# Third layer of a four-layer graph network: how the gathered rows are weighed, and how the ring that holds them is freed

## The chip, the cores and the metric

The kernel runs on one core of one Trainium2 chip. The metric is the device time of one execution in microseconds (us); the kernel before takes 5078.98 us, the median of three runs between 5077.45 and 5080.45. The engines are called by the names of the profile: PE is TensorE (PEld its weight loads), DVE is VectorE, ACT is ScalarE, POOL is GpSimd, SP is SyncE. "DVEq" is the part of VectorE that handles waits, registers and semaphores ahead of the arithmetic.

## The reference

3125 nodes with 128 features go through four graph layers over 50000 edges. The change touches the first half of the third layer, attention with eight heads of 64 features:

```python
def gat_layer(x, W, a, src, dst, n_nodes, concat):
    h = x @ W
    f = h.shape[-1]
    s_src = h @ a[:f]
    s_dst = h @ a[f:]
    score = s_src[src] + s_dst[dst]
    edge_e = jnp.exp(-jax.nn.leaky_relu(score, ALPHA))
    rowsum = jax.ops.segment_sum(edge_e, src, num_segments=n_nodes)
    msg = jax.ops.segment_sum(edge_e[:, None] * h[dst], src, num_segments=n_nodes)
    h_prime = msg / (rowsum[:, None] + EPS)
    return jax.nn.elu(h_prime) if concat else h_prime

heads = [gat_layer(x, W1[i], a1[i], src, dst, N, True) for i in range(W1.shape[0])]   # 8 heads
x_ = jnp.concatenate(heads, axis=1)
h = gat_layer(x_, W2, a2, src, dst, N, False)
```

For each edge the row h[dst] of every head is fetched, multiplied by that head's exp(-leaky_relu(score)), and added to the sums of node src. A column of ones in each head's row lets the same sum give the row sum: 8 x 65 = 520 values are summed, and eight values s_dst ride along, so that a record has 528 float32.

## The kernel before

The 3125 nodes are padded to 25 blocks of 128. An earlier stage has sorted the edges into a table of 416 slot rows of 128 lanes each (`SLOT_ROWS` = 416): in a slot row every lane holds one edge, and all of them belong to one block of nodes, whose number stands in `chunk_row`. `attend_rows` goes through this table once, in one block in which the five engines run side by side and wait for each other by semaphores. Within an engine the order is the one that the Python text writes out; there is no planner.

- POOL (L2053) gathers one slot row after the other by an indirect DMA into `got`, a ring of 3 buffers of 13 rows. Before it refills a buffer it waits (`free`) until DVE has added the whole set of 13 rows that lay in it.
- DVE makes the logits of a set of 13 rows in `leak` (L2127, L2128), after a wait for all 13 gathers; ACT takes the exponential (L2186); DVE multiplies by `live` in `mask` (L2135), which zeroes empty lanes. The results are the weights `factor`, in SBUF.
- Each row is then weighed in place: ACT multiplies heads 0 and 1, one ACTIVATE each (L2204), and DVE heads 2 to 7 in one operation of 390 values (L2142, `scale`). DVE adds the weighed row of 520 values to the block `y` that the row's chunk number selects (L2166). The add waits for the row's two multiplications (`scaled`, `weighed`) and for the add before it (`added`), because two rows can go to the same block.
- DVE's order is: scale of row t+1, add of row t, scale of row t+2, add of row t+1, and so on. `leak` of the next set stands before row 7 of a set, `mask` before row 12. At the start of each set `reg_load` (L2150) fetches 13 chunk numbers from `chunk_row` into registers; it follows a wait for all adds of the set before.
- Beside this, the same block transposes a matrix of edge counts for later layers: SP fetches pieces of `ct` (800 KB each, 25 of them), PE transposes 128x128 blocks (L2090) and counts degrees (L244), ACT copies each transposed strip out of PSUM (L2193, `flip`, one after every third row, 125 in all), and SP stores 25 pieces to `cs`. In ACT's order a flip stands between the rows, so an ACT that waits for PE in a flip does not weigh rows.

The first layer's rounds (L1607, L1664, L1673, L1681, L1698) do a similar job on rows of 516 values, with other lines of code: a ring freed by eights, register loads of eight, and adds that follow each other directly. They are not touched.

Part of the weighing in the text before:

```python
for r in range(ROWS):
    t = n * ROWS + r
    if n + 1 < SETS and r == 7:
        leak(n + 1)
    if n + 1 < SETS and r == ROWS - 1:
        mask(n + 1)
    if t + 1 < SLOT_ROWS:
        scale(t + 1)
```

## Time and profile before

| | |
|---|---|
| Median of three runs | 5078.98 us (5077.45 to 5080.45) |
| The profiled execution, its own time | 5069.63 us |
| Its span | 5067.9 us |
| Busy in the span | PE 1669.7, DVE 2841.0, ACT 1640.9, POOL 2024.4 us |
| The stage of the change, first gather to last add | 3448.8 to 4125.2 us |

The profile comes from one execution that is a little faster than the median. The stage of the change fills slices 28 to 33 of its 40, where DVE, ACT and POOL are all partly busy and PE's granted clock is at its lower level. A row of the timeline gives the start of an operation, its duration, engine, line, what it writes and reads, and in brackets the engine's idle time before it with the releaser that the profile infers; "issue" as releaser means that the engine waited for nothing that the profile shows, so a register load is hidden behind that word. Durations of neighbouring operations on DVE overlap a little; what an operation costs its engine is the distance from its start to the next start.

### The profile page before, as it was taken

Reading aid. Unit: us, or ns where it says so; the run is one execution under the profiler, and the core shown is the slowest. Engines: PE = TensorE matmul, PEld = TensorE weight load, DVE = VectorE, ACT = ScalarE, POOL = GpSimd, SP = SyncE. Lnnn points to the kernel's source line nnn. Section 1 sums busy time; section 2 is a strip of 40 time slices with the busy share of each in tenths; the row PEclk is TensorE's granted clock in tenths of the full one; section 3 lists DMA queues with packets and bytes.
Section 4 is the critical chain, followed back from the end, with each engine's and each line's share of the span. In section 5 each row is a group of like instructions: output and inputs, shape, how many; then the busy total and the mean of one; then the engine's idle time right before and its main releaser. Section 6 shows DMA issues by size and latency. Waiting matters only on the chain. (4 is left out here: it accounts for less than half of the span.)

```text
span 5067.9 us, 46827 instructions
## 1 busy us (share of the span) xinstructions
PE 1669.7 (33%) x10711; PEld 944.4 (19%) x10711; DVE 2841.0 (56%) x4778; ACT 1640.9 (32%) x4317; POOL 2024.4 (40%) x1847
## 2 busy tenths in 40 slices
PE   3133200100000000001543433522222237899989
PEld 2022200100000000000111111111111127644444
DVE  5728667781677779871333333564777775722131
ACT  1312301110656657001544333513444454310010
POOL 0055777706777710027123444126767642000000
PEclk9566555555555555555666665665555568999999
DMA  3000000005666620002011122226778736578856
GB/s 120 19 12 1 3 1 1 1 0 163 169 181 186 185 49 0 0 20 51 17 38 44 54 59 56 51 72 199 246 233 251 239 78 178 193 278 271 269 169 211
DMA packets 215383, 553.41 MB, mean 109 GB/s; under 512 B 46177, under 2 KB 112411, under 8 KB 214404
## 3 DMA queue, kind: packets, MB, share of 16 engines
q0 software_dynamic: 99984, 272.83, 19.9%
q1 hardware_dynamic: 115188, 278.18, 16.1%
q8 instruction: 82, 1.34, 0.1%
q14 instruction: 129, 1.06, 0.1%
HBM read 485.70 MB, written 65.20 MB: 109 GB/s over the span
## 5 line engine op out<-in xcount | busy, mean ns | idle before, releaser
L1171 POOL DMA_INDIRECT blend_got<-rec,blend_slot x416 | 394.8, 949 | 539.7 <-DVEq L1214 407.4
L900 POOL DMA_INDIRECT table<-edges_record,edges_place x391 | 512.8, 1311 | 142.9 <-issue 123.6
L2691 PE MATMUL fourth_bank<-fourth_tile,fourth_z 128*128 128x512 f16 (+1 forms) x2800 | 559.8, 361 | 19.8 <-DVEq L2852 10.1
L2053 POOL DMA_INDIRECT heads_got<-rec,heads_slot x416 | 466.8, 1122 | 183.8 <-issue 124.4
L244 PE MATMUL blend_count<-blend_mov,blend_stat 128*128 x980 | 351.2, 440 | 562.0 <-issue 461.6
L1607 POOL DMA_INDIRECT sum_got<-rec,sum_slot x416 | 456.9, 1098 | 157.3 <-issue 124.9
L1223 DVE TENSOR_SCALAR blend_mov<-built_iota_low,built_low 128x800 f16 x490 | 213.0, 435 | 516.2 <-issue 318.0
L1681 DVE TENSOR_TENSOR rounds_y<-rounds_y,sum_got 128x516 f32 x416 | 290.9, 699 | 124.7 <-issue 34.8
L1251 ACT ACTIVATE blend_gap<-built_iota_ten,built_offset 128x128 f32 x490 | 196.8, 402 | 493.4 <-issue 392.4
L200 PE MATMUL edges_p_key<-kept_ident,edges_key_row 128*128 128x128 f32 x4 | 1.1, 428 | 1035.6 <-DVEq L167 1035.6
L2691 PEld LDWEIGHTS fourth_bank<-fourth_tile,fourth_z 128*128 128x128 f16 x2800 | 261.7, 99 | 311.6 <-issue 15.0
L2166 DVE TENSOR_TENSOR third_a_y<-third_a_y,heads_got 128x520 f32 x416 | 288.6, 694 | 53.1 <-issue 35.1
L2142 DVE TENSOR_TENSOR heads_got<-heads_got,heads_factor 128x390 f32<-128x390 f32 x416 | 232.8, 560 | 111.8 <-issue 102.6
L1698 ACT ACTIVATE sum_got<-sum_got,edges_place 128x129 f32<-128x129 f32 x672 | 198.7, 387 | 265.2 <-issue 208.3
L244 PEld LDWEIGHTS blend_count<-blend_mov,blend_stat 128*128 x980 | 99.7, 102 | 822.1 <-issue 799.2
L2204 ACT ACTIVATE heads_got<-heads_got,heads_factor 128x65 f32<-128x65 f32 x832 | 217.2, 340 | 91.8 <-DVEq L2136 53.6
L1211 DVE SCALAR_TENSOR_TENSOR second_sums<-blend_got,blend_weight,second_sums 128x129 f32 x416 | 126.8, 351 | 157.3 <-issue 138.0
L1698 ACT ACTIVATE sum_got<-sum_got,sum_weights 128x129 f32<-128x129 f32 x576 | 169.4, 388 | 110.5 <-issue 55.1
L200 PEld LDWEIGHTS edges_p_key<-kept_ident,edges_key_row 128*128 128x128 f32 x4 | 0.7, 217 | 1036.3 <-issue 1036.3
L477 PE MATMUL once_bank<-kept_ident,once_e_rows 128*128 128x128 f32 x200 | 41.9, 393 | 421.4 <-issue 264.3
L1253 ACT ACTIVATE blend_stat<-blend_gap x490 | 151.6, 309 | 89.5 <-issue 39.8
L244 PE MATMUL heads_degrees<-heads_one,heads_flipped 128*128 128x1 f16 x625 | 41.0, 170 | 386.1 <-issue 162.4
(666 smaller groups left out, 4394.7 us busy)
## 6 DMA issues: line engine op xcount, KB each, us to landing
fourth_tile<-cs SPq DMA_DIRECT2D x100, 800.0 KB, 4.4
fourth_tile<-ct SPq DMA_DIRECT2D x100, 800.0 KB, 4.3
ct<-blend_cst SPq DMA_DIRECT2D x20, 1000.0 KB
heads_counts<-ct SPq DMA_DIRECT2D x25, 800.0 KB
cs<-heads_flipped SPq DMA_DIRECT2D x25, 800.0 KB
attend_cnt<-ct SPq DMA_DIRECT2D x50, 256.0 KB
sort_low_wide<-low SPq DMA_DIRECT2D x4, 3136.0 KB
attend_cnt<-ct SPq DMA_DIRECT2D x25, 288.0 KB
```

What stands on the lines that cost most here:

```text
L244: return pe.matmul(out, lhsT, rhs, start=False, stop=True, skip_group_check=True)
L900: pool.indirect_dma_start(table, bass.IndirectOffsetOnAxis(ap=K["place"][0:lanes, t:t + 1], axis=0), K["record"][0:lanes, t, :], None).the ...
L1171: pool.indirect_dma_start(got[:, buf, r, :], None, rec_dram, bass.IndirectOffsetOnAxis(ap=slot[:, t:t + 1], axis=0)).then_inc(gathered[buf ...
L1223: dve.tensor_scalar(at_slot(mov, at), K["iota_low"][:, :], K["low"][:, bass.ds(t, 1)], None, ALU.is_equal).then_inc(mov_ready, 1)
L1607: pool.indirect_dma_start(got[:, t % (HELD * PART), :], None, rec_dram, bass.IndirectOffsetOnAxis(ap=slot[:, t:t + 1], axis=0)).then_inc(g ...
L1681: dve.tensor_tensor(sums, sums, got[:, t % (HELD * PART), 0:heads * F1], ALU.add).then_inc(added, 1)
L1698: last = act.activation(part, part, ACT.Copy, scale=weights[half][:, k, r:r + 1])
L2053: pool.indirect_dma_start(got[:, buf, r, :], None, rec_dram, bass.IndirectOffsetOnAxis(ap=slot[:, t:t + 1], axis=0)).then_inc(gathered[buf ...
L2142: dve.tensor_tensor(part, part, factor[:, buf, r, ON_ACT:heads].unsqueeze(2).to_broadcast([P, heads - ON_ACT, F1]), ALU.mult).then_inc(sca ...
L2166: dve.tensor_tensor(out, out, got[:, buf, r, 0:WIDTH], ALU.add).then_inc(added, 1)
L2204: last = act.activation(part, part, ACT.Copy, scale=factor[:, buf, r, h:h + 1])
L2691: last = pe.matmul(bank[m][:, 0:w], z2[s % 2][:, k, part, :], tile[:, n % RING, at:at + w], start=(k == 0 and part == 0), stop=(k == NB - ...
```

## The change

- The ring becomes one of 40 rows in 5 parts of 8. POOL waits, before each part from the sixth on, for `added` to show that the part's old rows are summed; there is no `free` semaphore any more.
- A set is 16 rows (25 of them, and two of 8 at the end) instead of 13. `leak` has one add for each part of 8 rows and then the leaky step over the set; it stands before row 9 of a set of 16, `mask` before row 14.
- ACT weighs heads 0 to 2 (three ACTIVATEs for each row), DVE heads 3 to 7 of two rows in one operation of 650 values. `mask` is two operations: the weights of ACT's heads go to `factor` in SBUF as before, those of DVE's heads go to `across`, a part of the PSUM bank `p_slot`. `scale` reads its weights from there.
- DVE's order becomes: scale of rows r+2 and r+3, add of row r, add of row r+1.
- `reg_load` fetches 8 chunk numbers at every eighth row, and no wait for the adds stands before it.

```diff
-    BUFS, ROWS = 3, 13
-    SETS = SLOT_ROWS // ROWS
-    ON_ACT = 2
+    PART, HELD, ROWS = 8, 5, 16
+    SETS = [ROWS] * 25 + [PART, PART]
+    FIRST = [sum(SETS[:n]) for n in range(len(SETS))]
+    KEPT = 3
+    ON_ACT = 3
...
+    there = heads - ON_ACT
+    across = p_slot[:, 0:KEPT * ROWS * there].rearrange("p (u r h) -> p u r h", u=KEPT, r=ROWS)
...
-            for n in range(SETS):
-                buf = n % BUFS
-                if n >= BUFS:
-                    pool.wait_ge(free[buf], n // BUFS)
...
+            for part in range(SLOT_ROWS // PART):
+                if part >= HELD:
+
+                    pool.wait_ge(added, (part - HELD + 1) * PART)
+                for t in range(part * PART, (part + 1) * PART):
...
-                step(dve.tensor_tensor(l, own[:, :, at].rearrange("p h r -> p r h"), got[:, buf, :, WIDTH:WIDTH + heads], ALU.add))
+                l = logit[:, n % 2, 0:rows, :]
+                for part in range(first // PART, (first + rows) // PART):
+                    wait_gathered(dve, part)
+                    at = slice(part * PART, (part + 1) * PART)
+                    step(dve.tensor_tensor(l[:, part * PART - first:(part + 1) * PART - first, :], own[:, :, at].rearrange("p h r -> p r h"),
+                                           got[:, held(part * PART, PART), WIDTH:WIDTH + heads], ALU.add))
...
+                step(dve.tensor_tensor(e[:, :, 0:ON_ACT], e[:, :, 0:ON_ACT], alive.to_broadcast([P, rows, ON_ACT]), ALU.mult))
                 dve.sem_inc(factors, 1)
+                step(dve.tensor_tensor(across[:, n % KEPT, 0:rows, :], e[:, :, ON_ACT:heads], alive.to_broadcast([P, rows, there]), ALU.mult))
+
+            def scale(n, r):
+
+                part = got[:, held(FIRST[n] + r, 2), ON_ACT * F1:WIDTH].rearrange("p r (h f) -> p r h f", f=F1)
+                dve.tensor_tensor(part, part, across[:, n % KEPT, r:r + 2, :].unsqueeze(3).to_broadcast([P, 2, there, F1]),
+                                  ALU.mult).then_inc(scaled, 2)
...
+            for n, rows in enumerate(SETS):
+                for r in range(rows):
+                    t = FIRST[n] + r
+                    if r % PART == 0:
+                        dve.reg_load(regs, chunk_row[0:1, t:t + PART])
+                    if n + 1 < len(SETS) and r == rows - 7:
                         leak(n + 1)
+                    if n + 1 < len(SETS) and r == rows - 2:
                         mask(n + 1)
+                    if r % 2 == 0 and r + 2 < rows:
+                        scale(n, r + 2)
+                    elif r % 2 == 0 and n + 1 < len(SETS):
+                        scale(n + 1, 0)
...
-                    dve.wait_ge(scaled, t + 1)
+                    dve.wait_ge(scaled, t // 2 * 2 + 2)
                     dve.wait_ge(weighed, t + 1)
                     if t >= 1:
                         dve.wait_ge(added, t)
...
-                dve.wait_ge(added, (n + 1) * ROWS)
-                dve.sem_inc(free[buf], 1)
+            dve.wait_ge(added, SLOT_ROWS)
...
-                if n >= BUFS:
-                    act.wait_ge(free[n % BUFS], n // BUFS)
+                rows = SETS[n]
+                if n >= KEPT:
+                    act.wait_ge(added, FIRST[n - KEPT + 1])
...
-                    if n + 1 < SETS and r == 9:
+                    if n + 1 < len(SETS) and r == rows - 5:
                         exps(n + 1)
```

## Rows read from the trace of the kernel before

**Rows 1.** Stage's middle: busy us of PE, PEld, DVE, ACT, POOL; clock; DMA share.
```profile
3504.00:4091.00 587.00, 134.66 (x1790) 101.65 (x1790) 439.89 (x842) 266.08 (x913) 426.66 (x377) 0.50 0.79 240
```

**Rows 2.** Groups of instructions, 3440 to 4130 us: busy and mean ns, idle before.
```profile
L2053 POOL DMA_INDIRECT heads_got<-rec,heads_slot x416 | 466.8, 1122 | 183.8 <-issue 124.4 <-DVEq L2168 51.3 <-DVEq L2113 8.1
L2166 DVE TENSOR_TENSOR third_a_y<-third_a_y,heads_got 128x520 f32 x416 | 288.6, 694 | 53.1 <-issue 35.1 <-ACT heads_got L2204 16.9 <-DVE third_a_y L2166 0.2
L2142 DVE TENSOR_TENSOR heads_got<-heads_got,heads_factor 128x390 f32<-128x390 f32 x416 | 232.8, 560 | 111.8 <-issue 102.6
...
L2127 DVE TENSOR_TENSOR heads_logit<-third_a_own,heads_got 128x104 f32<-128x104 f32 x32 | 10.3, 323 | 24.0 <-DMA heads_got<-rec,heads_slot 24.0
```

**Rows 3.** Third layer's register loads, by line: count, min/median/max ns.
```profile
L2150 DVEq TENSOR_LOAD <-heads_chunk_row x32: 1094/2946/6077, 3469.4 to 4107.9; - x32
```

**Rows 4.** Timeline of DVE, one set of 13 rows of the third layer.
```profile
3541.19 0.69 DVE L2166 TENSOR_TENSOR third_a_y<-third_a_y,heads_got 128x520 f32 x1
3545.01 0.56 DVE L2142 TENSOR_TENSOR heads_got<-heads_got,heads_factor 128x390 f32<-128x390 f32 x1 [3.12 <-issue]
...
3546.16 0.55 DVE L2142 TENSOR_TENSOR heads_got<-heads_got,heads_factor 128x390 f32<-128x390 f32 x1
3546.64 0.69 DVE L2166 TENSOR_TENSOR third_a_y<-third_a_y,heads_got 128x520 f32 x1
...
3552.67 0.32 DVE L2127 TENSOR_TENSOR heads_logit<-third_a_own,heads_got 128x104 f32<-128x104 f32 x1
...
3553.44 0.57 DVE L2142 TENSOR_TENSOR heads_got<-heads_got,heads_factor 128x390 f32<-128x390 f32 x1
...
3558.89 0.26 DVE L2135 TENSOR_TENSOR heads_factor<-heads_factor,heads_live 128x104 f32<-128x104 f32 x1
3559.30 0.57 DVE L2142 TENSOR_TENSOR heads_got<-heads_got,heads_factor 128x390 f32<-128x390 f32 x1
```

**Rows 5.** Timeline of ACT: rows and flips, then a flip that waits.
```profile
3662.72 1.54 ACT L2204 ACTIVATE heads_got<-heads_got,heads_factor 128x65 f32<-128x65 f32 x6
3664.17 0.67 ACT L2193 COPY heads_flipped<-heads_p_own 128x640 f16<-128x640 f16 x1
3664.74 1.55 ACT L2204 ACTIVATE heads_got<-heads_got,heads_factor 128x65 f32<-128x65 f32 x6
...
3719.14 0.69 ACT L2193 COPY heads_flipped<-heads_p_own 128x640 f16<-128x640 f16 x1 [10.75 <-PE heads_p_own L2090]
```

**Rows 6.** First layer's register loads, by line.
```profile
L1673 DVEq TENSOR_LOAD <-sum_chunk_row x52: 594/596/614, 1273.2 to 1868.5; - x52
```

**Rows 7.** Timeline of DVE in the first layer: adds in a row, load behind one.
```profile
1430.53 0.73 DVE L1681 TENSOR_TENSOR rounds_y<-rounds_y,sum_got 128x516 f32 x1 [0.21 <-DVE rounds_y L1681]
1431.20 1.24 DVE L1664 TENSOR_TENSOR sum_got<-sum_got,sum_weights 128x1032 f32<-128x1032 f32 x1
```

**Rows 8.** Timeline of DVE: the third layer's last two adds.
```profile
4123.54 0.69 DVE L2166 TENSOR_TENSOR third_a_y<-third_a_y,heads_got 128x520 f32 x1
4124.47 0.70 DVE L2166 TENSOR_TENSOR third_a_y<-third_a_y,heads_got 128x520 f32 x1 [0.24 <-DVE third_a_y L2166]
```

**Rows 9.** Timeline of DVE at the stage's start; L2111 reads one operand from PSUM.
```profile
3447.26 0.59 DVE L2111 TENSOR_TENSOR heads_live<-heads_p_reach,heads_when 128x416 f32<-128x416 f32 x1 [1.45 <-PE heads_p_reach L2061]
...
3467.88 0.33 DVE L2127 TENSOR_TENSOR heads_logit<-third_a_own,heads_got 128x104 f32<-128x104 f32 x1 [18.49 <-DMA heads_got<-rec,heads_slot]
...
3471.01 0.69 DVE L2166 TENSOR_TENSOR third_a_y<-third_a_y,heads_got 128x520 f32 x1
```

**Rows 10.** Timeline of POOL, two gathers of the third layer.
```profile
3545.51 0.94 POOL L2053 DMA_INDIRECT heads_got<-rec,heads_slot  x1 [0.30 <-issue]
3546.75 1.39 POOL L2053 DMA_INDIRECT heads_got<-rec,heads_slot  x1 [0.30 <-issue]
```

**Rows 11.** Timeline: a PSUM operand on DVE beside a second-layer gather.
```profile
2283.13 0.59 DVE L1191 TENSOR_TENSOR blend_weight<-blend_p_weight,blend_live 128x416 f32<-128x416 f32 x1
2283.31 0.99 POOL L1171 DMA_INDIRECT blend_got<-rec,blend_slot  x1 [9.48 <-DVEq L1190]
```

More of the change, by code:

```diff
@@ L2018, in attend_rows, with wait_gathered, held @@
     scaled, weighed, added = c.sem("scaled"), c.sem("weighed"), c.sem("added")
-    gathered, free = [c.gather_sem(f"gathered{k}") for k in range(BUFS)], [c.sem(f"free{k}") for k in range(BUFS)]
+    gathered = [c.gather_sem(f"gathered{k}") for k in range(HELD)]
+    def wait_gathered(eng, part):
+        eng.wait_ge(gathered[part % HELD], (part // HELD + 1) * 16 * PART)
+    def held(first, count):
+        return slice(first % (HELD * PART), first % (HELD * PART) + count)
     with nc.Block() as block:
@@ L2131, in mask @@
             def mask(n):
-                e = factor[:, n % BUFS, :, :]
+                rows, first = SETS[n], FIRST[n]
+                e, alive = factor[:, n % KEPT, 0:rows, :], live[:, first:first + rows].unsqueeze(2)
                 dve.wait_ge(exped, n + 1)
-                step(dve.tensor_tensor(e, e, live[:, n * ROWS:(n + 1) * ROWS].unsqueeze(2).to_broadcast([P, ROWS, heads]), ALU.mult))
+                step(dve.tensor_tensor(e[:, :, 0:ON_ACT], e[:, :, 0:ON_ACT], alive.to_broadcast([P, rows, ON_ACT]), ALU.mult))
@@ L2136, in mask @@
                 dve.sem_inc(factors, 1)
-            def scale(t):
-                buf, r = (t // ROWS) % BUFS, t % ROWS
-                part = got[:, buf, r, ON_ACT * F1:WIDTH].rearrange("p (h f) -> p h f", f=F1)
-                dve.tensor_tensor(part, part, factor[:, buf, r, ON_ACT:heads].unsqueeze(2).to_broadcast([P, heads - ON_ACT, F1]),
-                                  ALU.mult).then_inc(scaled, 1)
+                step(dve.tensor_tensor(across[:, n % KEPT, 0:rows, :], e[:, :, ON_ACT:heads], alive.to_broadcast([P, rows, there]), ALU.mult))
@@ L2195, in _ @@
             exps(0)
-            for n in range(SETS):
-                buf = n % BUFS
+            for n, rows in enumerate(SETS):
                 act.wait_ge(factors, n + 1)
-                for r in range(ROWS):
-                    if n + 1 < SETS and r == 9:
+                for r in range(rows):
+                    t = FIRST[n] + r
+                    if n + 1 < len(SETS) and r == rows - 5:
                         exps(n + 1)
                     for h in range(ON_ACT):
-                        part = got[:, buf, r, h * F1:(h + 1) * F1]
-                        last = act.activation(part, part, ACT.Copy, scale=factor[:, buf, r, h:h + 1])
+                        part = got[:, t % (HELD * PART), h * F1:(h + 1) * F1]
+                        last = act.activation(part, part, ACT.Copy, scale=factor[:, n % KEPT, r, h:h + 1])
                     last.then_inc(weighed, 1)
-                    after = n * ROWS + r - FIRST_FLIP
+                    after = t - FIRST_FLIP
                     if after >= 0 and after % 3 == 0 and after // 3 < TURNS:
```

35 lines of the change are left out of this document (11 added, 24 removed).

## The prediction

> **What bounds the kernel now.** The page's slices come first: the change touches one stage, 3448.8 to 4125.2 us, and the stages after it wait for its last add, so what the stage loses or gains moves the end one for one. In the stage's middle, 587 us, DVE is busy 440, POOL 427, ACT 266 and PE 135, with the DMA engines at 0.79 [rows 1]. No engine is full, so the second view is who waits. POOL shows 0.30 us before nearly each gather, which is its own cost of issuing, and 51.3 us of waiting for a freed buffer; its period is 1.12 + 0.30 = 1.42 us, 592 us for 416 rows [rows 2]. DVE waits for gathers 24.0 us in all, before the first two sets [rows 2], so POOL's free waits are a consequence. DVE has 102.6 us of idle time before its scales, named "issue", in 32 pieces, and 53.1 us before its adds, where the weights of ACT come late [rows 2]. The 32 pieces are the 32 register loads: median 2.95 us, up to 6.08 [rows 3], and the timeline shows one as 3.12 us of nothing between two sets [rows 4]. DVE is the bound.
>
> The ledger of DVE from its first add (3471.0 [rows 9]) to the end of the last (4125.2 [rows 8]), 654 us:
> - rows: start to start 1.085 us (six rows from 3546.16 to 3552.67 [rows 4]), of which scale to add 0.48 and add to scale 0.61; 416 x 1.085 = 451.
> - per set after the first, `leak` 0.77 (3552.67 to 3553.44) and `mask` 0.41 (3558.89 to 3559.30) [rows 4]: 31 x 1.18 = 37.
> - register loads 103; waits before adds 53 [rows 2]; a wait for the second set's gathers 5.5, what is left of 24.0 after the first set's 18.5 [rows 2, 9].
> - sum 649; 5 us stay unexplained and are carried along.
>
> **The change part by part.**
>
> *Rows.* A DVE operation costs its engine about its elements at 1.04 ns plus 0.07 us (0.48 us for 390 values, 0.61 for 520 [rows 4]). 650 values are then 0.75 us for two rows, 0.37 instead of 0.48 a row. That is the visible gain, 43 us in all, but it changes the order: two adds now stand next to each other, and each waits for the add before it. Today a scale lies between, and the wait costs nothing. The last two adds of the stage are the one place where no scale is left, and there the second starts 0.93 us after the first instead of 0.61, with 0.24 idle [rows 8]; the first layer pays 0.21 before each add in the same way [rows 7]. So a pair costs 0.75 (scale) + 0.93 (add to add) + 0.61 = 2.29 us, 1.145 a row, against 1.085: 208 x 2.29 = 476, **+25 us**. Bounds: 0.61 instead of 0.93 would give -42; I see no reason for it, since the wait is kept.
>
> *Weights in PSUM.* The trace has an operation of 416 values with a PSUM operand at 0.59 us [rows 9]; between 390 values at 0.560 and 520 at 0.694, all in SBUF [rows 2], 416 would take 0.587. I take no extra cost. Bounds: nothing, and, since no row has a broadcast PSUM operand, half rate, 0.68 us x 208 = +141.
> The Trainium skill (VectorE: DVE Perf Modes, "The TRN2 errata — SBUF-src ops pay a fixed extra latency per instruction") gives 58 cycles plus size from SBUF and 120 from PSUM at 0.96 GHz. By that the 208 scales would take 13 us more. The row just quoted does not show it in the duration.
>
> *Leak and mask.* A set of 16 has two small adds, the leaky step, and two masks. From today's 0.36 and 0.41 I take 0.32 + 0.32 + 0.60 for the leak with the register work before the next add, less the 0.32 that the adjacent adds would have lost anyway: 0.93; the mask 0.41 becomes 0.64. 26 x 1.57 = 41, **+4 us**. Bounds 0 and +15.
>
> *Register loads.* 52 of 8 instead of 32 of 13. Today the load stands behind a wait for all adds, so DVE is empty while it runs. After, it is issued behind an add that still runs. The first layer has that very form: 52 loads of 594 to 614 ns [rows 6], and after one the next operation starts 0.67 us behind the add's start, 0.06 more than the 0.61 [rows 7]. 52 x 0.06 = 3 us. But the third layer's loads vary from 1.09 to 6.08 us [rows 3], beside transfers that the first layer does not have. If 4 in 10 of the 52 lengthen by 0.7 us (my estimate, about double their length, as 6.08 is to 2.95), that is 15 more. 103 - 18 = **-85 us**. Bounds: 3 us in all, or today's 3.2 us each, 167.
>
> *ACT.* Six ACTIVATEs and the step to the flip take 1.45 us, so 0.24 each, and a flip 0.57 (3664.17 to 3664.74) [rows 5]. A row goes from 0.48 + 0.19 = 0.67 to 0.91 us, still under DVE's 1.145: ACT is no bound on average. What shrinks is its lead. ACT may start a set only after `mask`. Today DVE then has one scale, an add, a load and a scale before it adds the new set's first row, about 5.2 us, and ACT is done with it after at most 1.5: lead 4, growing by 0.4 a row. After, DVE needs about 3.8 us to that add, ACT up to 1.7, so the lead is 2.1, growing by 0.24 a row. The lead hides stalls of ACT in a flip, when PE is late (10.75 us once [rows 5]). Of today's 53 us before adds, about 12 lie in the first sets and 40 behind such stalls. That is four or five of the size shown, and each costs 2 us more: **+10 us**. Bounds 0 and +40.
>
> *Start and ring.* The first set has 16 gathers instead of 13: 3 x 1.25 us later (0.95 + 0.30 [rows 10]), and a little more leak and mask: **+4 us**. The ring of 40 rows lets POOL run 32 to 40 rows ahead of the adds. `leak` now asks for rows 23 ahead of DVE; 8 rows or about 11 us of slack remain, enough for a stall of 10. I cost the ring at nothing, with POOL's spare time as cover (below).
>
> **Sum:** 25 + 4 - 85 + 10 + 4 = -42, and 2 back for moments in which POOL is the later one: **-40 us**. The profiled execution, 5069.6 us, becomes 5029.6; the median is 9.4 above the profiled one, so 5078.98 - 40 = **5039 us**.
>
> **Can POOL become the bound?** A gather lasts 0.945 us alone, and 1.39 when it starts while a DVE operation on two SBUF operands runs: the add of 3546.64 ends 0.58 us after the gather of 3546.75 starts, and 0.58 + 0.82 = 1.40 [rows 4, 10]. Beside the operation with a PSUM operand, of which 0.41 us were left, it took 0.99, not 1.23 [rows 11]. So the new scales no longer delay gathers, the adds do. Stepping gathers through a pair of 2.29 us (adds delay in about 0.94 us of it) gives delays of 0.54 us in five gathers, a period of 1.25 + 0.11 = 1.36. Then the last gather ends at 3448.8 + 415 x 1.36 + 1 = 4014, and after 3 us of transfer DVE still has 15 rows, 18 us: 4036. The DVE ledger ends at 4085. POOL is 49 us early: no bound.
> The Trainium skill (SBUF — State Buffer, "Who interferes with whom") says that two SBUF inputs contend with a GpSimd instruction that reads SBUF, and one does not: these rows agree. It also infers that `tensor_tensor` does not stall the generation of descriptors, which rows 10 contradict; by that inference the period would be 1.25, and POOL's end 46 us earlier.
>
> **Rivals.**
> - *DVE falls under POOL.* If loads hide fully (-15), ACT's lead suffices and its stalls are swallowed (-10 to -35), DVE meets POOL's end of 4036: -89, **4990 us**. For it: the ring is more elastic, stalls overlap gathers. Against it: PE's lateness is untouched, and DVE waits for it in order. Chance 0.15.
> - *ACT's lead is used up.* Three heads a row and a lead of 2.1 us: if each of 26 sets loses 1.3 us more behind a flip, +34: -6, **5073 us**, within the uncertainty. For it: 125 flips wait for PE, whose lateness may be more than the few long stalls. Against: the mean row of 0.91 leaves 0.23 us. Chance 0.12.
> - *The loads stay long* (the slower side). If what makes today's loads last 3 us is the place, not their form, 52 x 3.2 = 167 instead of 18: +109, **5188 us**. It decides from 58/52 = 1.1 us idle per load on. For it: rows 3. Against: rows 6 and 7, and that in the third layer the shortest is 1.09. With it goes half-rate PSUM, which decides from 0.19 us a scale. Chance 0.06.
>
> The forecast has 0.67. A change under 0.2%, 10 us, cannot be told from none. Faster: 0.67 + 0.15 and a quarter of 0.12, 0.85; the same 0.08; slower 0.07. The range that holds 8 in 10 goes from near the POOL case to the ACT case: 4992 to 5074.
>
> **What would show it.** Right: adds of odd rows 0.93 us behind those of even rows, with about 0.24 idle named after the add; scales near 0.83 us each and 208 of them; 52 loads near 0.6 us, with the idle time before scales fallen from 103 to under 25; gathers at a mean near 1.06 us; idle time before adds behind ACT of 50 to 60 us, beside some 50 of the add's own wait. Wrong: odd adds at 0.61 (then about -105), idle time before L2142's successor still over 60, scales over 1.0 us, or DVE waiting for gathers in most sets, which would make POOL the bound.

## The result and the profile after

The changed kernel takes 5096.97 us (median of 9 runs, 5088.91 to 5110.27), the kernel before 5077.45 us beside it (9 runs, 5066.92 to 5085.06): ratio 1.0043, 95% interval 1.0030 to 1.0055. It is slower by some 20 us; the forecast was 40 faster. The experiments ran on nine chips, and these fall into two groups: on three the kernel before takes 5037 to 5078 us, as on the chip of this comparison ("the first chip"), and on six 4366 to 4374 us. That difference bears on the miss, so it is told here.

The profiled execution of the changed kernel has a span of 5087.2 us. The stage, from the start of its first gather to the end of its last add (this is the measure of the stage everywhere below), takes 697.4 us (3446.8 to 4144.2) against 676.4 before (3448.8 to 4125.2 [rows 8]). The rest of the program is alike.

Groups by line in the stage after; columns as in [rows 2]:
```profile
L2063 POOL DMA_INDIRECT heads_got<-rec,heads_slot x416 | 425.7, 1023 | 235.7 <-issue 119.2 <-DVE third_a_y L2182 108.1 <-DVEq L2123 8.4
L2182 DVE TENSOR_TENSOR third_a_y<-third_a_y,heads_got 128x520 f32 x416 | 290.4, 698 | 188.0 <-issue 95.6 <-ACT heads_got L2220 34.7 <-DMA ct<-blend_cst 34.4
L2156 DVE TENSOR_TENSOR heads_got<-heads_got,heads_p_slot 128x650 f32<-128x650 f32 x208 | 172.0, 827 | 12.3 <-issue 9.4
L2139 DVE TENSOR_TENSOR heads_logit<-third_a_own,heads_got 128x64 f32<-128x64 f32 x52 | 13.4, 259 | 25.6 <-DMA heads_got<-rec,heads_slot 21.9 <-issue 2.3 <-DVE third_a_y L2182 0.7
```
Against [rows 2]: the scales are 208 of 827 ns, 172 us instead of 233; the idle time before them is 12.3 us instead of 111.8; the gathers are shorter, 1023 ns for 1122. Against that stands one number: 188.0 us idle before the adds, for 53.1. POOL, which was to be 49 us early, waits 108.1 us for adds (51.3 for freed buffers before): DVE is the bound, as forecast, but a longer one.

What the 188 us are, by DVE's waits (line waited for: us in all, times, longest):
```profile
DVE third_a_y L2182 <- issue: 95.6, 111, 4.4
DVE third_a_y L2182 <- ACT heads_got L2220: 34.7, 30, 10.0
DVE third_a_y L2182 <- DMA ct<-blend_cst: 34.4, 16, 4.2
DVE third_a_y L2182 <- DVE third_a_y L2182: 15.6, 65, 0.2
```
A DMA of `ct` cannot release an add, and ACT's late weights are the smaller part: for only 3 rows of 416 does ACT's last operation on the row end less than 0.35 us before the add, and the idle time before these three is 13.5 us. Such names are what ended last while something the profile doesn't name went on. The timeline of DVE shows it:
```profile
3605.19 0.70 DVE L2182 TENSOR_TENSOR third_a_y<-third_a_y,heads_got 128x520 f32 x1 [0.82 <-DVE heads_logit L2141]
3605.80 0.83 DVE L2156 TENSOR_TENSOR heads_got<-heads_got,heads_p_slot 128x650 f32<-128x650 f32 x1
3607.95 0.70 DVE L2182 TENSOR_TENSOR third_a_y<-third_a_y,heads_got 128x520 f32 x1 [1.33 <-issue]
3611.46 0.70 DVE L2182 TENSOR_TENSOR third_a_y<-third_a_y,heads_got 128x520 f32 x1 [2.80 <-ACT heads_got L2220]
3612.07 0.82 DVE L2156 TENSOR_TENSOR heads_got<-heads_got,heads_p_slot 128x650 f32<-128x650 f32 x1
3614.31 0.70 DVE L2182 TENSOR_TENSOR third_a_y<-third_a_y,heads_got 128x520 f32 x1 [1.42 <-issue]
3615.91 0.70 DVE L2182 TENSOR_TENSOR third_a_y<-third_a_y,heads_got 128x520 f32 x1 [0.90 <-DMA ct<-blend_cst]
```
For some 10 us the adds come with 1 to 3 us between them, then the pace is normal again for 30. In such a stretch DVE's small instructions (the register move, the address sum and the waits between two operations) take 0.70 us each. The move is one line of the program, so its group shows it (duration in ns, least/median/most). The changed kernel on the first chip, the kernel before on the same chip, the changed kernel on a chip of the other group:
```profile
L2175 DVEq MOVE  x402: 3/36/1386, 3506.6 to 4139.4; - x134
```
```profile
L2159 DVEq MOVE  x399: 36/36/36, 3507.8 to 4119.1; - x200
```
```profile
L2175 DVEq MOVE  x388: 36/36/36, 2870.5 to 3389.3; - x194
```
After the first 60 us of the stage the trace of the changed kernel has 114 moves, address sums and waits of 0.68 to 0.73 us on DVE, in 15 stretches some 40 us apart, and 122.9 of the 188.0 us before adds lie beside such an instruction (57 adds, the start of the stage included); the kernel before has none there, only one stretch at the start (3477 to 3503), with 12.5 us before adds. These "slow stretches" are what the experiments are about.

### The profile page after: what moved, and what is told of

It is laid out like the page before. It is cut to its first block and busy times, and to the rows that moved or that the text cites. A ratio compares the mean times of both kernels' runs of the same rounds, so it can differ in the third digit from the quotient of the medians.

```text
span 5087.2 us, 47089 instructions
## 1 busy us (share of the span) xinstructions
PE 1669.7 (33%) x10711; PEld 947.6 (19%) x10711; DVE 2821.3 (55%) x4607; ACT 1752.6 (34%) x4728; POOL 1988.8 (39%) x1847
## 5 line engine op out<-in xcount | busy, mean ns | idle before, releaser
L2063 POOL DMA_INDIRECT heads_got<-rec,heads_slot x416 | 425.7, 1023 | 235.7 <-issue 119.2
L2182 DVE TENSOR_TENSOR third_a_y<-third_a_y,heads_got 128x520 f32 x416 | 290.4, 698 | 188.0 <-issue 95.6
L2220 ACT ACTIVATE heads_got<-heads_got,heads_factor 128x65 f32<-128x65 f32 x1248 | 327.8, 341 | 100.0 <-issue 84.8
L2156 DVE TENSOR_TENSOR heads_got<-heads_got,heads_p_slot 128x650 f32<-128x650 f32 x208 | 172.0, 827 | 12.3 <-issue 9.4
```

The costliest lines, as they stand in the source:

```text
L2063: pool.indirect_dma_start(got[:, t % (HELD * PART), :], None, rec_dram, bass.IndirectOffsetOnAxis(ap=slot[:, t:t + 1], axis=0)).then_inc(g ...
L2182: dve.tensor_tensor(out, out, got[:, t % (HELD * PART), 0:WIDTH], ALU.add).then_inc(added, 1)
L2220: last = act.activation(part, part, ACT.Copy, scale=factor[:, n % KEPT, r, h:h + 1])
```

## The experiments

All ratios are to the kernel before on the same chip. "Stage" is from the profiled execution. The kernel before was profiled on the first chip and in run 6 only; on the chips of runs 12, 17 and 18 its stage is not known.

| run | what differs | median us | ratio (95%) | stage us |
|---|---|---|---|---|
| 6 | kernel before | 4369.6 | | 628.7 |
| 5 | changed kernel | 4327.67 | 0.9901 (0.9884-0.9917) | 588.5 |
| 4 | before + short loads | 4372.92 | 1.0005 (0.9996-1.0014) | 634.3 |
| 10 | before + PSUM weights | 4368.37 | 0.9987 (0.9977-0.9996) | 630.3 |
| 9 | changed, weights in SBUF | 4369.70 | 1.0001 (0.9991-1.0011) | 629.0 |
| 3 | changed, one row a scale | 4335.41 | 0.9925 (0.9911-0.9938) | 597.7 |
| 2 | changed, two heads on ACT | 4332.65 | 0.9914 (0.9901-0.9928) | 592.6 |
| 1 | changed, wait before each load | 4343.53 | 0.9942 (0.9928-0.9955) | 606.0 |
| 7 | changed + SyncE's waits | 4329.65 | 0.9911 (0.9895-0.9928) | 588.1 |
| 8, 14 | changed, odd rows with one wait | 4316.32, 4319.59 | 0.9877 (0.9861-0.9894), 0.9891 (0.9874-0.9908) | 582.2, 582.0 |
| 11, 15, 16 | as 8, two heads on ACT | 4334.38, 4328.01, 4326.32 | 0.9909 (0.9892-0.9925), 0.9912 (0.9896-0.9929), 0.9910 (0.9894-0.9927) | 591.1, 589.5, 592.6 |
| **chips with slow stretches** | | | | |
| first | kernel before / changed | 5077.45 / 5096.97 | 1.0043 (1.0030-1.0055) | 676.4 / 697.4 |
| 12 | changed, load of 16 behind a pause | 5104.26 | 1.0050 (1.0033-1.0067) | 703.1 |
| 13 | as 8 + SyncE's waits | 5106.03 | 1.0050 (1.0033-1.0066) | 718.4 |
| 17 | as 11, load of 16 behind a pause | 5071.45 | 1.0088 (1.0055-1.0120) | 685.6 |
| 18 | before + short loads + PSUM weights | 5066.51 | 1.0060 (1.0036-1.0085) | 684.6 |

### Runs 1 to 4: three theories for the stretches, and another chip

Theory 1: the old 3 us pause at each set's end let the instruction stream catch up. Theory 2: ScalarE's further instructions crowd it. Theory 3: two adds side by side starve it.

Run 1, before each of the 52 loads:
```
+                        if t >= 1:
+                            dve.wait_ge(added, t)
                         dve.reg_load(regs, chunk_row[0:1, t:t + PART])
```


> The changed kernel with one more wait: each of the 52 register loads stands behind the end of the add before it, as the 32 loads of the kernel before did. Theory 1 (the pause): VectorE's instruction stream falls behind because nothing in the new order lets it catch up; the old pause of 3 us at the end of each set did. Then the 16 stretches in which VectorE's waits and register moves take 0.70 us each go away or shrink to a few, the idle time in gaps of over 0.5 us before adds falls from 143 us to under 40, the drains cost 52 x 1.1 = 57 us in the gaps before scales, and the median comes to about 5010-5040 us. Theory 2 (ScalarE's 406 further instructions crowd out VectorE's) and theory 3 (two adds side by side) leave the stretches where they are: about 5097 + 57 = 5150 us.

Run 2: `ON_ACT = 2`.


> The changed kernel with ScalarE weighing two heads instead of three, VectorE six: 416 fewer ScalarE instructions, nothing else moved. 780 values per scale instead of 650 cost 0.13 us, 208 times, 27 us. Theory 2 (ScalarE's instructions crowd out VectorE's): the slow stretches go, -130 us, median about 4995 us. Theories 1 (the pause) and 3 (two adds side by side): the 16 stretches stay, idle before adds behind ScalarE falls by some 20 us at most: 5097 + 27 - 10 = 5115 us.

Run 3 (`across` is the weights' place in PSUM; not shown: the order of DVE becomes scale, add, scale, add again, and each add waits for its own row's scale):
```
-    dve.tensor_tensor(part, part, across[:, n % KEPT, r:r + 2, :] ... [P, 2, there, F1]).then_inc(scaled, 2)
+    dve.tensor_tensor(part, part, across[:, n % KEPT, r, :] ... [P, there, F1]).then_inc(scaled, 1)
```


> The changed kernel with the old order: one scale of one row (five heads, 325 values, weights in PSUM) between any two adds, all else as changed. By the durations a row is 0.34 + 0.07 = 0.41 us to the add and 0.61 behind it, 1.02 us against 1.145 for half a pair: -50 us of VectorE's ledger. Theory 3 (two adds side by side starve the sequencer): the slow stretches go as well, VectorE falls under GpSimd, median 4930-4990 us. Theory 1 (the pause) and theory 2 (ScalarE's instructions): the stretches stay, a few more of them since VectorE has some 100 more instructions: about 5050 us.

Run 4, on the kernel before (parts of the edit; POOL and ACT wait for the count of adds instead of `free`):
```
-                dve.reg_load(regs, chunk_row[0:1, n * ROWS:(n + 1) * ROWS])
...
+                    if t % 8 == 0:
+                        dve.reg_load(regs, chunk_row[0:1, t:t + 8])
...
-                dve.wait_ge(added, (n + 1) * ROWS)
-                dve.sem_inc(free[buf], 1)
```


> The kernel before (sets of 13 rows, three buffers, one row per scale, weights in SBUF, two heads on ScalarE) with only the register loads of the change: 52 of 8 rows, each issued behind an add that still runs, and no wait for all adds at the end of a set (GpSimd and ScalarE wait for the count of adds themselves). Theory 1 (the pause): the load's idle time falls from 103 to under 20 us, but the slow stretches appear about every 128 VectorE instructions, 15 or more of them, some +130 us: median about 5110-5130 us. Theories 2 and 3 (ScalarE's instructions; two adds side by side): no such stretches, median about 4990-5000 us.

None of the three theories was tested: on this chip the kernel before takes 4370.61 us, no engine of the four edited kernels shows such stretches in the stage, and all four expectations miss. What the runs show there: against run 5 below, another wait at each load costs some 16 us (run 1). Run 2 is 5 us and run 3 8 us slower than run 5, but they ran on another chip and the intervals of their ratios overlap with run 5's, so what the third head and the pairs are worth is not clear of the noise here. Run 4 is the instructive one: the idle time of the loads is gone, and nothing is gained, since 129.7 us of waiting for gathers stand in its place, before 29 sets of 32.

### Runs 5 and 6: the same two kernels on a chip without stretches

> The changed kernel, nothing edited, beside the kernel before on the chip of this job. In the chip of the first comparison VectorE's instruction stream had slow stretches (waits and register moves of 0.70 us) over the whole program, and the kernel before took 5077 us; in the chip of the four experiments the kernel before took 4371 us and the edited kernels show no such stretches. Theory A: the stretches are the whole of the miss. Where they are absent, VectorE's ledger is the predicted one and the change gains what was predicted or is caught by GpSimd: 4325 to 4345 us against 4371, ratio 0.990 to 0.994. Where they are present, the ratio is 1.004 again. Theory B: the miss lies in the change itself (the pairs of adds, ScalarE's third head): ratio 1.00 or over in either case.

> The kernel before, unedited, for its trace on this chip. Theory A: the stage of the third layer is as before in its own parts (scale 0.56 us, add 0.69, 32 register loads near 3 us, 103 us idle before scales), while in other stages the idle time that no semaphore explains falls: the 540 us before the second layer's gathers become about 150 as in the fourth experiment. Theory B: the third layer's loads are short here as well (under 1.5 us), and the 103 us were never the load's.

Theory A's expectation holds: 4369.75 to 4327.67 us, 42 us faster, 40.2 of them in the stage. The second layer, which the change does not touch, shows how the chips differ. POOL's gathers there, before on the first chip ([rows 11] are from that stage), before on this one:
```profile
L1171 POOL DMA_INDIRECT blend_got<-rec,blend_slot x416 | 394.8, 949 | 539.7 <-DVEq L1214 407.4
```
```profile
L1171 POOL DMA_INDIRECT blend_got<-rec,blend_slot x416 | 402.8, 968 | 150.5 <-issue 125.6
```
The third layer's stage of the kernel before (to be read with [rows 2]), then of the changed one, on this chip:
```profile
L2053 POOL DMA_INDIRECT heads_got<-rec,heads_slot x416 | 470.9, 1132 | 134.4 <-issue 126.4 <-DVEq L2113 8.0
L2166 DVE TENSOR_TENSOR third_a_y<-third_a_y,heads_got 128x520 f32 x416 | 287.9, 692 | 1.1 <-DVE third_a_y L2166 0.2
L2142 DVE TENSOR_TENSOR heads_got<-heads_got,heads_factor 128x390 f32<-128x390 f32 x416 | 232.4, 559 | 108.6 <-issue 99.5
L2127 DVE TENSOR_TENSOR heads_logit<-third_a_own,heads_got 128x104 f32<-128x104 f32 x32 | 10.3, 321 | 32.0 <-DMA heads_got<-rec,heads_slot 32.0
```
```profile
L2063 POOL DMA_INDIRECT heads_got<-rec,heads_slot x416 | 430.5, 1035 | 134.5 <-issue 120.9 <-DVEq L2123 8.0 <-DVE third_a_y L2182 5.5
L2182 DVE TENSOR_TENSOR third_a_y<-third_a_y,heads_got 128x520 f32 x416 | 290.6, 699 | 56.6 <-DVE third_a_y L2182 32.8 <-ACT heads_got L2220 12.9 <-DVE heads_logit L2141 10.9
L2156 DVE TENSOR_TENSOR heads_got<-heads_got,heads_p_slot 128x650 f32<-128x650 f32 x208 | 171.9, 827 | 16.2 <-issue 13.4
L2139 DVE TENSOR_TENSOR heads_logit<-third_a_own,heads_got 128x64 f32<-128x64 f32 x52 | 13.4, 257 | 47.2 <-DMA heads_got<-rec,heads_slot 46.7
```
Two things are seen. The 53.1 us before adds of [rows 2] are 1.1 here: ACT's lateness behind PE, and the stretch at the stage's start, belong to the first group of chips. And the changed kernel has the adds' own wait that the prediction worked out (56.6 us here for "some 50"), but none behind ACT.

### Runs 7 to 9: a common rate? an easier add, and what PSUM does

Run 7, before each of SyncE's 25 stores: `for _ in range(32): sp.wait_ge(loaded, 16)` (800 waits in the text; the trace has 369 more SyncE instructions).


> The changed kernel with 800 further waits on SyncE in the third layer's gather stage, all on a semaphore that has long been reached (32 before each of its 25 stores, some 0.05 us each). SyncE is idle there and nobody waits for it. Theory R (a common rate): on the first chip all engines together got 11.3 instructions per us in this stage, before (7636 in 676 us) and after (7897 in 697 us), and the miss is the 261 instructions more. On such a chip 800 more cost some 70 us: ratio to before 1.017 or over. Theory O (each engine's own stream): the stretches depend on VectorE's own instructions and their pauses, SyncE's change nothing: ratio 1.004. Where the stretches are absent both say 4325-4330 us, ratio 0.990.

Run 8, no stretches either:
```
-                    dve.wait_ge(scaled, t // 2 * 2 + 2)
-                    dve.wait_ge(weighed, t + 1)
+                    if t % 2 == 0:
+                        dve.wait_ge(scaled, t + 2)
+                        dve.wait_ge(weighed, t + 2)
```


> The changed kernel with VectorE's odd rows waiting for the add before alone, and the even rows for both rows' weighing by ScalarE (no wait is lost, two of six move from the odd row to the even one): 208 to 400 instructions fewer on VectorE, and ScalarE's lead one row (0.9 us) shorter. Without slow stretches: the lead was 1.08 us at its shortest and 1.8 at the tenth part, so some adds wait up to 0.5 us: 4325-4335 us, ratio 0.990-0.992. With them: theory R (a common rate) gives 208/11.3 = 18 us and more back, ratio 1.000 or under; theory O (VectorE's own stream) gives a tenth part of 143 us back, ratio 1.001-1.002, less what ScalarE's late rows then cost.

Run 9: the scale reads `factor[:, n % KEPT, r:r + 2, ON_ACT:heads]`, one mask for all eight heads.


> The changed kernel with the weights of VectorE's five heads kept in SBUF, where they were: the scale then has two SBUF operands, and one mask does the work of two. Theory P (the PSUM operand spares the gathers): gathers that start beside a scale last until its end plus 0.82 us, their mean goes from 1.035 to about 1.15 us, GpSimd's period to 1.44 us, and it becomes the bound by far: first gather to last add 600 + 31 = 630 us instead of 588, ratio 0.999-1.001 to before. Theory N (no such contention from the scales): the mean stays at 1.035, the scale at 0.83 us, the split mask saves 0.24 x 26 = 6 us: ratio 0.989.

Run 7 changes nothing, as both theories said for such a chip. Run 8 is faster than both kernels, 0.9877, and faster than expected (4316 us for 4325 to 4335); its four times lie under all four of run 7 on the same chip. An odd add starts 0.84 us after the even one instead of 0.93: part of the "own wait" goes with the two waits that the odd add no longer has. Idle before adds falls from 56.6 to 35.3 us, and 62.9 us of waiting for gathers replace 46.7: POOL bounds it now.
```profile
L2183 DVE TENSOR_TENSOR third_a_y<-third_a_y,heads_got 128x520 f32 x416 | 292.3, 703 | 35.3 <-DVE heads_logit L2141 8.8 <-DVE third_a_y L2183 0.7
L2139 DVE TENSOR_TENSOR heads_logit<-third_a_own,heads_got 128x64 f32<-128x64 f32 x52 | 13.3, 256 | 63.1 <-DMA heads_got<-rec,heads_slot 62.9
```
Run 9 settles PSUM for such a chip, as theory P expected. The scale is as long with its weights in SBUF (832 ns for 827), but the gathers are 1141 ns instead of 1035, 416 x 0.106 = 44 us of POOL, DVE's idle time before its leak sums is 97.8 us instead of 47.2, and the whole gain is gone:
```profile
L2063 POOL DMA_INDIRECT heads_got<-rec,heads_slot x416 | 474.6, 1141 | 134.4 <-issue 124.9 <-DVEq L2123 7.9 <-DVE third_a_y L2181 1.5
L2155 DVE TENSOR_TENSOR heads_got<-heads_got,heads_factor 128x650 f32<-128x650 f32 x208 | 172.9, 832 | 14.0 <-issue 9.6 <-DVE heads_factor L2149 0.5
```

### Runs 10, 11, 14, 15 and 16: two bounds close together

Run 10: the kernel before, its six heads' weights masked into PSUM.


> The kernel before with only the weights of VectorE's six heads moved to PSUM (one more mask in each of 32 sets); sets of 13 rows, 32 loads behind a pause, one row a scale, two heads on ScalarE. Theory M (two bounds close together): VectorE's ledger keeps its 99 us of loads and gains 32 x 0.25 = 8 us of masks, so freeing the gathers alone brings nothing but the 14 us that VectorE waited for them: ratio 0.998-1.001, gather mean 1.03-1.05 us against 1.13. Theory Q (PSUM is the gain by itself): the ratio falls to 0.993 or under. On a chip with slow stretches theory R (a common rate of 11.3 instructions per us) says +32 instructions and more, ratio 1.000-1.002.

Run 11: as run 8, with `ON_ACT = 2`.


> The eighth run's kernel (odd rows wait for the add alone) with ScalarE back at two heads, VectorE at six: the fewest instructions of all versions, about 620 under the changed kernel in this stage. Without slow stretches VectorE's scales are 0.135 us longer, 28 us, of which 63 us of waiting for gathers can take most: 4316-4326 us, ratio 0.988-0.990. With them theory R (a common rate) gives (7898 - 624)/11.3 = 644 us for the stage against 676 before, ratio 0.993-0.995, and theory O (VectorE's own stream, whose instructions fall by 208 of 2192) gives 1.000-1.003.

Theory M holds. In run 10 the gathers fall to 1024 ns, and POOL now waits 45.5 us for buffers, while the idle time before DVE's scales stays (106.5 us for 108.6). Short loads alone (run 4) or PSUM alone (run 10) bring 0.1% at most, since the other engine takes over at once; run 3, which has both (and the ring and the third head, but no pairs), gains 35. Run 10's rows:
```profile
L2055 POOL DMA_INDIRECT heads_got<-rec,heads_slot x416 | 426.2, 1024 | 173.5 <-issue 120.1 <-DVEq L2171 45.5 <-DVEq L2115 7.9
L2145 DVE TENSOR_TENSOR heads_got<-heads_got,heads_p_slot 128x390 f32<-128x390 f32 x416 | 230.6, 554 | 106.5 <-issue 100.8
```
Run 11 is slower than run 8 and than its expectation (4334 us for 4316 to 4326): its longer scales are paid although DVE waits 50.0 us for gathers. Runs 14 to 16 repeat 8 and 11 and met no chip with stretches, so theory R was not tried by them. Runs 14 and 15 are on one chip: there the third head on ACT is worth 8 us (4319.59 against 4328.01, times that do not overlap).


> The eighth run's kernel again (odd rows wait for the add alone), hoped for on a chip with slow stretches. There theory R (a common rate of 11.3 instructions per us) gives 7690/11.3 = 681 us for the stage against 676 before: ratio 1.000-1.002, and the difference to 718 us with SyncE's idle waits is theirs. Theory O (VectorE's own stream) has no reason for a difference from that run: ratio 1.005. Without slow stretches 0.988 again.

> The eleventh run's kernel again (odd rows wait for the add alone, two heads on ScalarE), the one with the fewest instructions, 7274 in the stage. On a chip with slow stretches theory R gives 7274/11.3 = 644 us, 32 less than before: ratio 0.993-0.995, the only version faster than the kernel before there. Theory O: as the run before it, since VectorE's instructions are the same 1983: 1.003-1.006. Without slow stretches 0.991 again.

> The kernel with the fewest instructions once more (odd rows wait for the add alone, two heads on ScalarE; 7274 in the stage), for a chip with slow stretches. Theory R (a common rate of 11.3 per us): 644 us for the stage, ratio 0.993-0.995. Theory O (VectorE's own stream, 1983 instructions as in the run with SyncE's waits, which gave 1.005): 1.003-1.006. Without slow stretches 0.991 a third time.

### Runs 12 and 13: a chip with stretches

Run 12, instead of a load of 8 at each `r % PART == 0`:
```
+                    if r == 0:
+                        if t >= 1:
+                            dve.wait_ge(added, t)
+                        dve.reg_load(regs[0:rows], chunk_row[0:1, t:t + rows])
```


> The changed kernel with the register loads as the kernel before had them in place: one load of a whole set's 16 registers, behind the end of the set's last add, 27 in all. On a chip without slow stretches: if the length of a load goes by its registers (2.95 us for 13), 27 loads of 3.6 us cost 97 us of idle time instead of 16, 4385-4400 us, ratio 1.004-1.006; if it is the odd start of a set of 13 that made them long, a load of 16 takes about 1.2 us, 27 x 1.3 = 35 us: 4340-4350 us, ratio 0.994. On a chip with slow stretches theory O (VectorE's own stream needs a pause to catch up) says that they go and the idle time before adds falls from 188 to under 60 us; theory R (a common rate) says that they shrink only as far as the rate falls: some 11.3 instructions per us in the stage as before.

Run 13: run 8's kernel with run 7's waits on SyncE.


> The eighth run's kernel (odd rows wait for the add alone) with the 800 idle waits on SyncE of the seventh. Without slow stretches: nothing, 4316 us, ratio 0.988, as the eighth run. With them: theory R (a common rate of 11.3 per us) gives (7898 - 208 + 800)/11.3 = 751 us for the stage, 75 more than before, ratio 1.015; theory O gives 0.998-1.002.

The kernel before takes 5078.12 us here, and the stretches are back: 85 small DVE instructions of 0.70 us in run 12 after the first 60 us of the stage, in spite of a pause at each of 26 sets. Theory O's expectation fails: idle before adds is 166.7 us, not under 60. The load of 16 registers has a median of 1.10 us, as expected if the odd start of a set was what made loads of 13 long.
```profile
L2184 DVE TENSOR_TENSOR third_a_y<-third_a_y,heads_got 128x520 f32 x416 | 290.2, 698 | 166.7 <-issue 78.2 <-DMA ct<-blend_cst 38.1 <-ACT heads_got L2222 28.3
L2156 DVE TENSOR_TENSOR heads_got<-heads_got,heads_p_slot 128x650 f32<-128x650 f32 x208 | 171.9, 827 | 43.2 <-issue 39.0 <-DVE third_a_y L2184 1.4
L2168 DVEq TENSOR_LOAD <-heads_chunk_row x27: 4/1099/3655, 3477.7 to 4146.9; - x27
```
Run 13's ratio, 1.0050, misses both theories' ranges (1.015; 0.998 to 1.002). By the counts of the traces theory R looked right even so: 7636, 7898, 7873 and 8059 instructions of all engines in 676.4, 697.4, 703.1 and 718.4 us, 11.2 to 11.3 per us four times. In run 13 SyncE has stretches as well: 111 of its waits take 0.70 us.

### Runs 17 and 18: two more chips with stretches

Run 17: run 11's kernel with run 12's load.


> The kernel of the eleventh run (odd rows wait for the add alone, two heads on ScalarE) with one register load of 16 behind the end of a set's last add, 27 instead of 52: 7249 instructions in the stage. On a chip with slow stretches theory R (a common rate of 11.3 per us) gives 642 us and a ratio of 0.993-0.995, theory O (VectorE's own stream) 1.003-1.005. Without slow stretches: 26 pauses of 1.10 + 0.1 us, 31 us idle before scales instead of 8, of which the 50 us of waiting for gathers takes up most: 4328-4345 us, ratio 0.991-0.995. If a load of 16 took 3.6 us there (by its registers), it would be 4385 us, ratio 1.004.

Run 18: the kernel before with the edits of runs 4 and 10; neither ring of 40, nor pairs, nor third head.


> The kernel before with two parts of the change, PSUM weights (six heads, one row a scale) and 52 loads of 8 registers with no pause; sets of 13, three buffers and two heads on ScalarE stay. Theory M (two bounds close together): on a chip without slow stretches VectorE's ledger is 607 - 99 - 32 + 10 + 8 = 494 us and GpSimd's 416 x (1.07 + 0.30) = 570: GpSimd bounds, first gather to last add about 600 us against 629, ratio 0.993-0.995. If pairs and ring were needed as well, 1.000. On a chip with slow stretches: if they belong to the pairs and the ring, VectorE shows none after the first sets and the ratio is 0.993-0.997; if they come with the missing pauses or a denser stage whatever its form, 1.003 or over.

Run 17 fails theory R's forecast: 7249 instructions in 685.6 us, 10.6 per us, 1.0088 where 0.993 to 0.995 was expected. Here DVE's stretches are few (42 small instructions of 0.70 us), but it waits 47.4 us for ACT, seven times, up to 9.7, and ACT's flips wait 104.0 us with no releaser named but "remote". Run 18 (7658 instructions, 11.2 per us again) says what is enough for stretches on DVE: the pauses taken away and the gathers freed, together. It has the order, the sets, the ring and the two heads of the kernel before, and 120 small instructions of 0.70 us in 13 stretches after the first 60 us. Which of its two parts brings them is open: neither run 4's nor run 10's kernel has a trace on such a chip. Its rows:
```profile
L2170 DVE TENSOR_TENSOR third_a_y<-third_a_y,heads_got 128x520 f32 x416 | 289.1, 695 | 134.9 <-issue 100.8 <-ACT heads_got L2207 23.4 <-DMA ct<-blend_cst 9.6
L2145 DVE TENSOR_TENSOR heads_got<-heads_got,heads_p_slot 128x390 f32<-128x390 f32 x416 | 230.1, 553 | 19.2 <-issue 12.2 <-DVE third_a_y L2170 1.3
L2129 DVE TENSOR_TENSOR heads_logit<-third_a_own,heads_got 128x104 f32<-128x104 f32 x32 | 10.3, 322 | 29.3 <-DMA heads_got<-rec,heads_slot 25.2 <-issue 3.4 <-DVE third_a_y L2170 0.6
```
Add up DVE's idle time before its leak sums, scales and adds on chips with stretches. Before [rows 2]: 24.0 + 111.8 + 53.1 = 189 us. Run 18: 29 + 19 + 135 = 183. The changed kernel: 26 + 12 + 188 = 226, less some 45 that are the pairs' own wait: 181. Run 12: 24 + 43 + 167 = 234, less 45: 189. On a chip without stretches the same sums are 142 us before and 120, less 50, after. The first four are alike, but they come from different chips, and runs 17 and 13 have 188 and 244, less some 35 for their form of the wait, so the sum is no law. Beside each other on one chip stand only the medians: run 18 is 29 us slower than the kernel before (5037.34 us).

## Why the prediction was wrong

The ledger of DVE can be read from the traces term by term, from the start-to-start times of its operations and the idle time before them (changes in us, rounded):

| term | forecast | first chip | run 6 to run 5 |
|---|---|---|---|
| rows, with the pairs' own wait | +25 | +23 | +26 |
| leak and mask | +4 | +10 | +10 |
| loads (idle before scales) | -85 | -99 | -92 |
| idle before adds that start 0.2 us after ACT's last weight | +10 | -26 | 0 |
| idle before adds beside small DVE instructions of 0.70 us | no term | +110 | 0 |
| first add later | +4 | +4 | +4 |
| waits for gathers after the first add | +2 | -2 | +11 |
| stage | -40 | +21 | -40 |

*The step that failed is "Register loads ... 103 - 18 = -85 us"*, as a term that shortens the stage by itself, on the chip where it was to hold. The idle time at the loads fell even further than said (111.8 to 12.3 us before scales), but DVE's small instructions then took 0.70 us in stretches, which the sum has no term for: 12.5 us of idle time before adds became 122.9. Gaps of over 0.5 us there went from 52 us (15 of them) to 143 us (69). The prediction asked what a long load costs and what it collides with; it did not ask whether DVE's instructions would keep up without the pause. That idle time taken from the loads can come back before the adds is shown by run 18, which takes away the pauses and frees the gathers: 19.2 us before scales and 134.9 before adds, where the kernel before has 111.8 and 53.1 on the first chip. That it is the missing pauses, and not the denser stage as a whole, is not shown; why the shorter pauses of run 12 do not help is open.

*"ACT waits, 40 becomes 50, +10"* failed too. The reading of the trace before was right: 9 adds start 0.2 us after ACT's last weight, with 39.4 us of idle time before them, and the name "issue" hides four of the nine. The longest but one:
```profile
4022.84 0.69 ACT L2193 COPY heads_flipped<-heads_p_own 128x640 f16<-128x640 f16 x1 [10.72 <-issue]
4023.43 1.55 ACT L2204 ACTIVATE heads_got<-heads_got,heads_factor 128x65 f32<-128x65 f32 x6
4024.22 0.70 DVE L2166 TENSOR_TENSOR third_a_y<-third_a_y,heads_got 128x520 f32 x1 [9.50 <-issue]
```
After the change it is 3 adds and 13.5 us on the first chip, and none in run 5 or run 6, so this wait goes with chips with stretches and not with the length of ACT's lead. The rival built on the lead did not come about: the longest wait for ACT in run 5 is 0.6 us.

The other steps, in run 5 against run 6:
- *Rows +25.* Odd adds start 0.93 us after even ones with 0.24 idle, the next even one 1.36 later (medians): 2.29 us a pair, as worked out.
```profile
3005.43 0.82 DVE L2156 TENSOR_TENSOR heads_got<-heads_got,heads_p_slot 128x650 f32<-128x650 f32 x1
3006.18 0.69 DVE L2182 TENSOR_TENSOR third_a_y<-third_a_y,heads_got 128x520 f32 x1
3007.11 0.70 DVE L2182 TENSOR_TENSOR third_a_y<-third_a_y,heads_got 128x520 f32 x1 [0.24 <-DVE third_a_y L2182]
```
- *PSUM 0.* 827 ns in PSUM, 832 in SBUF (run 9).
- *Loads -85.* 108.6 to 16.2 us before scales: -92. Of the 52 loads 41 take 0.59 to 0.62 us and 11 take 1.2 to 2.3, 13 us longer in all; the estimate had 15.
- *Leak and mask +4.* +10: 5.7 in the operations, 4.2 of idle time before the second mask.
- *POOL.* Period 1.035 + 0.29 = 1.33 us for 1.36 forecast, its end 557 us after the stage's start for 565. But it is no 49 us early: DVE waits 46.7 us for gathers, half of it in the first sets. The prediction's two bounds were nearer to each other than it said.
- *Sum.* 628.7 - 588.5 = 40.2 us in the stage, 42 in the median, for 40 forecast. That it fits so closely is partly luck: the loads gave 7 us more and ACT's 10 us did not come, and against them leak and mask cost 6 more and the gathers 9 more.

So the ledger was near on a chip without stretches and 60 us off on the chip at hand. The trace held warnings that were not used: in the second layer POOL sat idle for 539.7 us before its gathers, 407.4 of them behind DVE's queue, and at the start of the third layer's stage 16 small DVE instructions took 0.70 us each.

## What to carry to other kernels

Before a pause is taken out of an engine's stream, look whether its small instructions ever take 0.70 us in the same program: then the stream, not the work, may set the pace, and a saving in idle time must be shown on such a chip, not only summed. Compare kernels on more than one chip before a change of 1% is believed (0.9901 on one and 1.0043 on another in this case). Where two engines have nearly the same ledger, relieve both or expect nothing (runs 4, 9 and 10); and give the second of two dependent operations as few waits of its own as correctness allows (run 8).

## What the runs showed of the hardware

- *The same program takes 15 to 16% longer on some chips.* The kernel before takes 5037 to 5078 us in the first comparison and on three chips of the experiments, and 4366 to 4374 on six. On the first group small instructions take 0.70 us in stretches: 299 on DVE, 268 on ACT and 305 on PE in the whole trace of the kernel before, against 3, 1 and 1 in run 6. The stretches of the engines often coincide: in the changed kernel's stage on the first chip DVE's cover 154 of the last 637 us and hold 61 of ACT's 107 us of idle time named "issue", and 153 of PE's 305. The second layer's gathers take 925 us for 544. The Trainium skill (Runtime: NRT & Kernel Launch, "Instruction fetch mechanics") says that the next block of instructions is fetched while the current one runs and that this is mostly hidden. Run 6, with 3 such instructions on DVE, fits that. That the stretches of the first group are late instruction blocks is a guess, and no run shows it: on DVE they begin 105 to 164 instructions apart after the change and 107 to 201 in run 18, and the instruction transfers themselves do not differ. The stage of the kernel before has 15 of 16 KB and 30 of 8 KB on either group, mean 1.10 and 0.36 us on the first chip, 1.05 and 0.37 in run 6.
- *A register load's length goes by where it starts.* Of the 32 loads of 13 each fourth takes 1.10 us, and these begin at a multiple of four values (set 4k begins at 52k); the others take 2.94 or more (run 6; on the first chip one of the eight took 2.64). The loads of the third and the fifth set (values 26 and 52 on), in run 6:
```profile
L2150 DVEq TENSOR_LOAD <-heads_chunk_row x1: 2983/2983/2983, 2873.8 to 2873.8; - x1
...
L2150 DVEq TENSOR_LOAD <-heads_chunk_row x1: 1109/1109/1109, 2911.0 to 2911.0; - x1
```
  Loads of 8 at multiples of 8 have a median of 0.60 us (run 5), and of 16 at multiples of 16 one of 1.10 (run 12). Some are longer even so, 11 of 52 in run 5, and no run shows why. The prediction weighed place, form and transfers and missed the start.
- *Gathers are shorter when DVE's scales read one operand from PSUM.* 1141 to 1035 ns (run 9 against run 5), 1132 to 1024 (run 6 against run 10); the only other difference is one mask more in each set.
